# A two-layer block with routed experts on one core: the five hand-written step orders replaced, TensorE's fillers dropped

## The chip, the core and the metric

The kernel runs on one core of a Trainium2 chip. The metric is the device time of one execution in microseconds. The engines are TensorE (PE), VectorE (DVE), ScalarE (ACT), GpSimd (POOL) and SyncE (SP), which here only starts DMAs; each works through its own instructions in program order and meets the others at semaphores.

## What is computed

The input is 32 x 256 tokens of width 128 (8192 rows, float32). Six residual layers follow each other, each on the layer-normed sum so far:

```
x = x + 0.5 * ffn0(layernorm(x))     # 8 experts, top 2 of a softmax gate, plus a shared expert
x = x + attn0(layernorm(x))          # linear attention, 32 heads of 4, group norm
x = x + 0.5 * ffn0(layernorm(x))     # the same weights again
x = x + 0.5 * ffn1(layernorm(x))     # 8 experts, top 1
x = x + attn1(layernorm(x))          # gated recurrence over 256 tokens, 8 heads, rope
x = x + 0.5 * ffn1(layernorm(x))
```

The expert of ffn0 is `a = swiglu((x w1 + b1) * (x w3 + b3))`, `y = a w2 + b2`, and each token adds the y of its two experts, weighted by the gate.

## The kernel before

**Tiling.** x stays in the core's memory. It is cut into 16 chunks of 512 tokens (4 tiles of 128), and the chunks into three groups of 4, 6 and 6 for ffn0. A group's tokens are sorted by expert: POOL writes every token's row twice to a DRAM table (`scatter`, L1593, two indirect transfers a tile), at the places that the routing has counted. The table is then read in units of 512 sorted rows, four blocks of 128 that each have one expert: 10 units in group 0, 14 in groups 1 and 2. SP loads a unit by four transposing DMAs (`load_rows`, L1660) into one of five buffers `u_xp`; PE, ACT and DVE compute the unit; ACT copies its result and SP stores it to DRAM (L1677); POOL fetches two results for each token by indirect transfers (`fetches`, L1610, eight a chunk), into one of two buffers, and DVE adds them to x (`weighed`, L963).

**Steps.** The work is cut into steps, and each step has an index k that says which part of it an engine does. In this text: h l.c.k is step k of `head` for layer l (0 the first ffn0, 1 the attention and the second ffn0) and chunk c: in layer 1, k = 0 adds the fetched results and takes the statistics, 1 and 2 take the attention's mean and normalise by `rstd`, 3 to 10 are the attention, 11 on the second ffn0 (11 statistics, 12 normalise, 13 rows, 14 logits and half of the shared expert). In the layer's steps before ffn0 DVE's L920 and L924 make mean and variance, POOL's L1562 and L1564 make `rstd`, DVE's L931 normalises with it. r l.b.k is the routing of a pair of chunks (b), U l.g.u.k is unit u of group g: k = 1 and 2 are PE's products (L652, L659), which ACT widens and DVE multiplies (L1208, L1193, L1197), k = 3 is DVE's last product (L1201), k = 4 is PE's product with w2 (L670, L673), ACT's copy and SP's store. S l.g.t is a scatter, F l.c.n a fetch. The later layers are steps m and l (ffn1 before and after the second attention) and f and b (that attention, front and back).

**What sets the order.** Nothing in the loops does. The dictionary `turns` (L380) has a string for each of the five engines, a letter for each step; `order` (L513 on) takes for each letter the next step of its kind, and the engine's program does its part of that step, or nothing. Even units are u, odd ones w; heads a, b, c by chunk modulo 3. So an engine that meets a step whose input isn't there stands still, with all that its string has behind it. The letter z, on PE alone, is a filler: `warm` (L894) multiplies the identity by itself, 256 columns, into a place that nobody reads. The string before has 462 of them.

**SP's own steps.** At the start of a group (`experts`, k = 0 of unit 0) SP clears the ends of the experts' regions by eight small DMAs (L1645) and loads units 0, 1 and 2 in one step; k = 1 of unit u loads unit u + 3; k = 4 stores unit u. Before the load of unit 0 it waits for all scatters of the group (`scattered`) and for the cleared ends. `Waiting.wait_ge` remembers the highest value waited for on each semaphore and emits a wait only for a higher one.

Of the kernel before, what the change touches and what calls it, by code (L numbers as in the profile page):

```python
# [24 lines left out]
E = 8  # L25
# [110 lines left out]
def build(nc, dram, packed, x_in, out):  # L136
# [14 lines left out]
    with ExitStack() as ctx:  # L151
# [225 lines left out]
        for i, which in enumerate("abc"):  # L377
# [4 lines left out]
                "aazzzzzzzzzzzzzzzzzzzzzzzzzzzzzzzzzzzzzzzzzzzzzzzzzzzzzzzzzzzabbzzzzzzzzbcczzcaabbcaaarrrrbbbcbbbccc"  # L382
                "aaabbabbbaccczccaaarrrrrbbbcccbrrrbaaazzzzzzzzzzzzzzzzarrrrrbbbcccaccaaazzzzzzzzzzzzzzzzzzzuwrrrrrzz"
                "zzzzzuubbbwcccwuuzzzzzzzuzuwwaaazzwucccwwbbuuuwwuzwuwcuuwbbbuczauwwaucccwwzwuurrrrraazzzauubbbuwzzwa"
                "aarrrbzzzzzwzaabrrrrruuwbbbcccaaawcurrrrrcwwuuwwzzwcccaaauuawwawuurrrrrwuzwaaauuuuurrrwwwaaaawauuuaw"
                "bbbbauzzzzzzzzzzzzzzzzzzabaccccwwbubcazabuucwbucuuaaabbacazcwaazzawuubbbbbwwccuaaaabbbwarrrrrzzzwawc"
                "ccaucwwazzzcawuwcczcaauuzuwwwuaaauzaauuwaaawwrrrrrrrrzzzzzzzzzzzzzzzzzzzzzzuwwzzzuwuuuwuwzzuwwuwwuuw"
                "uwwwuuzzzwuuwbbbbubzzuwzzwzuwbbwbuuubccccaaaawbbcuwwucbbbcbwbcacuuwwbbbuwwccauuwawwacccuuucabbbzzbcu"
                "wwucccaawrrrrrbbaaauuwbawbccccabcwwaaazzubbcwuuwcwcuuubbbbbcwwuaaaaccubbbrrrrraawacccuuuwcwaabbbbzzc"
                "baaubcccbwwuaaawuzzzzzzubaabwwccccbbaaaucrrrrrwwczzzzzzzuuwbbbcwcbuurrzzzzzzzzrcbwbbzbaaaazauccawwuw"  # L390
# [11 lines left out]
            "vector": (
                "acbabacbcaabarabbrrbacarcbbabcbcacbrcbabcbrbbacbracarccbcrraarrcrbabcracrbabrcabrrrabcacrrbacrbarcuu"
                "uuccacwwwawcuuuuwwwwubwbbuuuubuccwwwbwcawracruuubuaurcbawwwwrarabrwauuuaucrrbuarcbrararcbrbrabwwwrra"
                "acwcwcarcruuuawwwuucwwaraarruuurrrwwwauuaaawwuuuarurbubaawwwbaccawacwuuubbaabubuaccbcabcabauuuubabca"
                "cauababaawwwcwbrawbrbbrcbcaacarcwwwwrwauuucacccauauawwwacwwaauuuuauaraarrrrwwwarrwwuuuuuwwwwwuuuuuww"
                "wrbwwuuucbuucbwwwwwabbuuuaubcbuabbwwwbwbbccwbbuuucbucubcbaacbwwwcwwbbccbuuuaucacwwwuawbcrwacrcacruuu"
                "caaruauabbcbrcwwwacbabwbwaabccaababcuuuuubcwwwbcawbrbwcrcbbrcuuucubaarcaucbrbwwwcaacbawabbcacabuuuwc"
                "acauubcbaacrbabrawwwrwbawbccrrbcbuuurucabcuabwwwrcbbrabcbwaawcccbauuucuabcurwwwcaccararcwaarbbwabacb"
                "rcabuuuabacbauwwwubabaccbwbcwacuuuuabbcrcubrcaabrbwwwccrawcwcruuuamcaucuaccwwwwamcuuuwaauaunnawwwwuu"  # L410
                "uuaurwaarararruuurrurwwwuwwmwwwuuuwwummunwwwmmmnnwmtmwmtmttttnnnmmuuunttnuwwwuwtttntwnttvtvuuuvvvvmm"
                "mluuttmwwwmttwwnnlmvtmtllttuuutuvunnnttvvvvonllltlowwwmmwwnuuuuuoovvnwwwtwuuunooovvvvulwtuoltttlltnn"
                "ttwwwtwwvlllvuuuluvvvvmmmoumotmwwwmwoowtmoootttuuuotuunnnttmmnwwwnwntwntvtmmmttvtmtmmvvvvttnnlttlmtl"
                "lttttnnnmmnvttvnnllltvvvvtonlovnnvttootttvvvvmmmllmttooonnnlltmtmvonnlllmvntltntmmvvvvtotmmmnnttottm"
                "tmtmootttvooomnnnottvttvvvvlvltnntmmttvtllnttvvvvnotlllommmnntlmmtmootmtttooonnnttvonnvnntvvvvltvltm"
                "mtnntttllnnnttnlllvttvvvvoltotmmmtmttvoottvttooovvvvtltlotvttllttvttlllvvvvototltvttoovtttooovvvvvvl"
                "lovvvvollooolllooolouw"
# [1203 lines left out]
        def sync_program(sp):  # L1621
            on = Waiting(sp)
# [373 lines left out]
```

## Time and profile before

| | |
|---|---|
| runs | 1545.92 us median of 3 (1544.52, 1545.92, 4823.48) |
| the profiled execution | 1546.17 us |
| its span, first to last instruction | 1544.2 us |
| mean granted TensorE clock | 0.922 of full |
| busy: PE, DVE, ACT, POOL | 84%, 75%, 48%, 43% |

The span is what the views below are made of; 1.97 us of the profiled execution lie around it. PE's records are matmuls whose ends are modelled, so a busy PE is not PE at its peak. Engines work in order: the number in square brackets behind a row is the time that the engine stood idle before it, and what it was released by. In a view by windows, each engine has its busy microseconds and its instructions in the stretch, then the granted clock, the DMA share and the GB/s.

### The profile page before, as it was taken

Reading aid. Unit: us, or ns where it says so; the run is one execution under the profiler, and the core shown is the slowest. Engines: PE = TensorE matmul, PEld = TensorE weight load, DVE = VectorE, ACT = ScalarE, POOL = GpSimd, SP = SyncE. Lnnn points to the kernel's source line nnn. Section 1 sums busy time; section 2 is a strip of 40 time slices with the busy share of each in tenths; the row PEclk is TensorE's granted clock in tenths of the full one; section 3 lists DMA queues with packets and bytes.
Section 4 is the critical chain, followed back from the end, with each engine's and each line's share of the span. In section 5 each row is a group of like instructions: output and inputs, shape, how many; then the busy total and the mean of one; then the engine's idle time right before and its main releaser. Section 6 shows DMA issues by size and latency. Waiting matters only on the chain.

```text
span 1544.2 us, 40929 instructions
## 1 busy us (share of the span) xinstructions
PE 1297.2 (84%) x15013; PEld 993.3 (64%) x15013; DVE 1153.2 (75%) x3632; ACT 737.0 (48%) x1226; POOL 671.2 (43%) x727
## 2 busy tenths in 40 slices
PE   1567987598876986888898899999998999999998
PEld 0434765476655765566676777777776776767776
DVE  5888698679746785788998675866678678787775
ACT  0344454235422443442554345565577547456572
POOL 0056646774457354766677514211235234130100
PEclk9987998799987988898999997999999989999999
DMA  8002423331133213321333321111111001000000
GB/s 279 0 30 68 111 60 93 101 92 52 62 93 104 71 48 82 82 65 51 95 92 100 80 72 53 38 43 49 36 39 31 21 22 32 16 20 9 9 16 22
DMA packets 171811, 94.21 MB, mean 61 GB/s; under 512 B 98411, under 2 KB 163078, under 8 KB 171366
## 3 DMA queue, kind: packets, MB, share of 16 engines
q1 hardware_dynamic: 151814, 54.19, 13.4%
q0 software_dynamic: 16384, 33.59, 7.4%
q10 hardware_dynamic: 3424, 3.81, 0.8%
q8 instruction: 130, 2.13, 0.6%
q14 instruction: 59, 0.48, 0.1%
HBM read 25.98 MB, written 45.61 MB: 46 GB/s over the span
## 4 chain that ended last, share of the span: by engine, by line
PE 44%; DVE 25%; issue 9%; POOL 7%; SPq 6%; ACT 5%; DMA 2%; POOLq 0%; DVEq 0%
PE bank L659 5%; SPq L1660 5%; PE bank L716 4%; POOL y_in L1610 3%; POOL rows L1593 3%; PE bank L693 2%; PE bank L743 2%; PE bank L673 2%; PE bank L530 2%; PE bank L873 2%; PE sums L890 2%; DVE heads_store L931 2%; PE bank L652 2%; DVE heads_store L1011 2%; DVE x L963 1%
## 5 line engine op out<-in xcount | busy, mean ns | idle before, releaser
L1610 POOL DMA_INDIRECT y_in<-ys,r_result x256 | 274.3, 1071 | 156.1 <-issue 69.5
L1593 POOL DMA_INDIRECT rows<-store,r_slot x256 | 262.7, 1026 | 106.4 <-issue 75.6
L659 PE MATMUL bank<-u_xp,w_hi 128*128 128x128 f16 x2432 | 252.6, 224 | 2.2 <-DMA u_xp<-rows 2.0
L659 PE MATMUL bank<-u_xp,w_lo 128*128 128x128 f16 x1216 | 232.0, 223 | 0.0
L659 PEld LDWEIGHTS bank<-u_xp,w_hi 128*128 x2432 | 198.7, 100 | 48.8 <-issue 9.0
L652 PE MATMUL bank<-r_member,by_expert 128*128 128x512 bf16 x304 | 120.0, 395 | 12.1 <-DVE u_linear_odd L1208 9.2
L659 PEld LDWEIGHTS bank<-u_xp,w_lo 128*128 x1216 | 121.4, 100 | 0.7
L963 DVE SCALAR_TENSOR_TENSOR x<-y_in,r_weight,x 128x128 f32<-128x128 f32 x256 | 72.6, 345 | 21.6 <-DMA y_in<-ys,r_result 20.5
L1407 ACT ACTIVATE heads_store<-bank,b3s,sc 128x512 f32<-128x512 f32 x64 | 49.4, 776 | 77.5 <-PE bank L530 77.0
L530 PE MATMUL bank<-heads_store,w_hi 128*128 128x512 f16 x256 | 82.8, 408 | 3.5 <-ACT u_linear_odd L1459 1.4
L716 PE MATMUL bank<-w_packed,heads_store 128*128 128x128 f32 x512 | 80.7, 303 | 0.9 <-DVE heads_store L1239 0.9
L1562 POOL TENSOR_SCALAR ve_last<-mv_last 128x4 f32<-128x4 f32 x16 | 3.8, 236 | 173.2 <-DVE mv_last L924 173.2
L716 PEld LDWEIGHTS bank<-w_packed,heads_store 128*128 128x128 f32 x512 | 74.0, 207 | 6.2 <-issue 1.8
L1562 POOL TENSOR_SCALAR ve_head<-mv_head 128x4 f32<-128x4 f32 x48 | 10.2, 212 | 143.2 <-DVE mv_head L924 141.5
L904 PE MATMUL sums<-w_ident_b 128*128 128x256 bf16 x362 | 57.4, 301 | 17.2 <-DVE own_region L1871 17.2
L931 DVE TENSOR_SCALAR heads_store<-x,mv_head,rstd_head 128x128 f32<-128x128 f32 x192 | 54.9, 359 | 22.3 <-POOL rstd_head L1564 22.3
L1379 ACT COPY heads_store<-bank 128x512 f32<-128x512 f32 x64 | 37.6, 587 | 69.1 <-PE bank L481 58.7
L693 PE MATMUL bank<-heads_store,f_w1s 128*128 128x512 f32 x128 | 69.5, 668 | 0.7 <-DVE heads_store L1228 0.6
L670 PE MATMUL bank<-by_expert,r_member 128*128 128x128 bf16 x304 | 32.3, 234 | 41.8 <-DVE u_linear_odd L1201 24.8
L1562 POOL TENSOR_SCALAR ve_front<-mv_front 128x4 f32<-128x4 f32 x16 | 3.1, 192 | 137.2 <-DVE mv_front L924 136.7
L1354 DVE TENSOR_TENSOR store<-store,bank 128x512 f32<-128x512 f32 x64 | 40.9, 680 | 27.2 <-PE bank L873 17.8
L1011 DVE SCALAR_TENSOR_TENSOR heads_store<-bank,b1s,heads_store 128x512 f32<-128x512 f32 x64 | 47.6, 744 | 12.7 <-ACT heads_store L1407 10.5
(340 smaller groups left out, 3468.1 us busy)
## 6 DMA issues: line engine op xcount, KB each, us to landing
ys<-u_y_even SPq DMA_DIRECT2D x38, 256.0 KB
ys<-u_y_odd SPq DMA_DIRECT2D x38, 256.0 KB
u_xp<-rows SPq DMA_TRANSPOSE x304
x<-x_dram SPq DMA_DIRECT2D x16, 256.0 KB, 7.2
rows<-store,r_slot POOLq DMA_INDIRECT x256, 2.3
y_in<-ys,r_result POOLq DMA_INDIRECT x256
out_dram<-x SPq DMA_DIRECT2D x16, 256.0 KB
rows<-blank SPq DMA_DIRECT2D x48, 64.0 KB, 1.6
```

The lines of the kernel that those rows point to most:

```text
L530: ins = pe.matmul(B[:], wp[:, m, :], s.xp[:, xp, :], start=(n == 0), stop=(n == 2))
L652: pe.matmul(B[:], by_expert[:, 2 * part + which, :], members(use).unsqueeze(2).broadcast_to([P, PER_UNIT, BLOCK]), start=True, stop=False, ...
L659: ins = pe.matmul(B[:, of_block[j]], of_expert(wp, e, 2 * part + which), xp_rows[:, xp, of_block[j]], start=False, stop=(n == 2 and j == P ...
L693: s.by_tensor.mark(pe.matmul(B[:], f1_w1s[:, j * P:(j + 1) * P], s.xt, start=True, stop=True), "gelu", c, j)
L716: pe.matmul(Y[:, by_t[t]], s.gs[j][:, by_t[t]], const["f1_w2"][:, j, :], start=(t == 0 and j == 0), stop=False, skip_group_check=True)
L904: pe.matmul(into, ident_b[:], ident_b[:, 0:HALF].unsqueeze(1).broadcast_to([P, T, HALF]), start=True, stop=True, skip_group_check=True)
L931: ins = dve.tensor_scalar(out[:, t, :], xc(c)[:, t, :], s.mv[:, t, 0:1], s.rstd[:, t:t + 1], ALU.subtract, ALU.mult)
L963: ins = dve.scalar_tensor_tensor(xt, y[:, t, i, :], w[:, i, t0 + t:t0 + t + 1], xt, ALU.mult, ALU.add)
L1011: s.by_vector.mark(dve.scalar_tensor_tensor(h, ring[s.name, "h", l, c, part, 1][:], b1s[:, part:part + 1], h, ALU.add, ALU.mult), "h", l, ...
L1593: pool.indirect_dma_start(row_dram[g], bass.IndirectOffsetOnAxis(route.slot[g][:, i, t:t + 1].bitcast(U32), 0), rows[:, groups[g].first * ...
L1610: pool.indirect_dma_start(fetch.y[i][:, t, k, :], None, y_dram[g], bass.IndirectOffsetOnAxis(route.result[g][:, k, t0 + t:t0 + t + 1].bitc ...
L1660: sp.dma_start_transpose(unit_xp[i % XP_BUFFERS][:, :, of_block[j]], block_rows(row_dram[g], firsts[j])).then_inc(rows_in[i % XP_BUFFERS], 16)
```

## The change

All five strings are replaced. A program that reads the letters as `order` does finds the same steps on each engine, each once, in another order: of the steps that have work on the engine, 654 of 890 stand at another place on PE (by 1.7 places in the mean), 883 of 1094 on DVE, 572 of 816 on ACT, 436 of 496 on POOL and 94 of 156 on SP. PE's string has 2 letters z where it had 462. And `load_rows` has its two waits at every unit:

```diff
-                if u == 0:
-                    on.wait_ge(scattered[g], 16 * 2 * groups[g].tiles * (l + 1))
-                    on.wait_ge(cleared[g], 16 * (1 + E * (l + 1)))
+                on.wait_ge(scattered[g], 16 * 2 * groups[g].tiles * (l + 1))
+                on.wait_ge(cleared[g], 16 * (1 + E * (l + 1)))
```

The strings, cut to the first lines of two of them:

```diff
             "tensor": (
-                "aazzzzzzzzzzzzzzzzzzzzzzzzzzzzzzzzzzzzzzzzzzzzzzzzzzzzzzzzzzzabbzzzzzzzzbcczzcaabbcaaarrrrbbbcbbbccc"
-                "aaabbabbbaccczccaaarrrrrbbbcccbrrrbaaazzzzzzzzzzzzzzzzarrrrrbbbcccaccaaazzzzzzzzzzzzzzzzzzzuwrrrrrzz"
+                "acaacburbbcaabaabccrbarbcbbbcarcrbaabcrcbaarbrabbraracbcrwbcabrrcrcbarcrbabcacaabrcbbrcrcuabuawruawc"
+                "urcauucwwwucbruwbubuwucrwbuwwubrcbcawwauawucuwaurarwrucbwrrwuawbuuacrubwcrcbaurrruacarwwawbbaraucrrw"
...
             "sync": (
-                "uuwwuuuuuwwwwwuuuwwwuuwwuuuuuwwwuuuwwwwwuuuuuuuwwwwwwwuuuuuwwwwwuuuuuwwwwwuuuuuwwwwwuuuuuuuuuuwwwwww"
+                "uuuwwwwuwuwuwuuuuwuwwuwuwwwuuuuuwwwuwuuowuwwuwwuwuwwuwwuwuouwuuuwwuuwuuuuuwwwuuwwuwwwuwowuwwwwwuuuu"
```

Read as steps with work, the places that the prediction speaks of (- before, + after; "load 0-2" is the step that clears and loads three units; "load 3" is U k = 1 of unit 0, and so on):

```
SP, start of group 1, layer 0   - load 0-2, load 3, store U0.0.9, load 4
                                + load 0-2, store U0.0.9, load 3, load 4
SP, start of group 2, layer 0   - load 0-2, load 3, store U0.1.13, load 4
                                + load 0-2, store U0.1.13, load 3, load 4
SP, start of group 0, layer 1   - load 0-2, load 3, store U0.2.13, load 4
                                + load 0-2, store U0.2.13, load 3, store U1.0.0
SP, start of group 1, layer 1   - load 0-2, store U1.0.9, load 3, load 4
                                + load 0-2, load 3, store U1.0.9, store U1.1.0
SP, start of group 2, layer 1   the same: load 0-2, load 3, store U1.1.13

POOL, F0.0.0 to F0.0.7          - 5 scatters of group 2 in between;  + 2
POOL, F0.7.0 to F0.9.7          - 8 steps of h, no scatter in between;  + 9 steps of h, 11 scatters
POOL, around F0.10.0            - S1.1.6 S1.1.7 h1.9.1 F0.10.0 h1.7.11 F0.10.1
                                + F0.9.7 S1.1.4 S1.1.5 h1.7.11 F0.10.0 ... F0.10.5 h1.9.1

DVE, end of group 1, layer 0    - U0.1.12.3 h1.3.15 r1.1.0 h1.3.16 h1.3.17 r1.1.1 r1.1.2 r1.1.3 r1.1.4
                                  U0.1.13.1 h1.3.18 r1.1.5 r1.1.6 U0.1.13.2 U0.1.13.3 U0.2.0.1
                                + U0.1.12.3 r1.0.4 h1.3.11 h1.2.17 h1.3.12 U0.1.13.1 h1.3.13 U0.1.13.2
                                  U0.1.13.3 h1.3.14 r1.1.0 h1.3.15 r1.1.1 h1.3.16 r1.1.2 U0.2.0.1
PE, the same place              - U0.1.13.2 r1.1.3 r1.1.6 22 fillers U0.1.13.4 3 fillers U0.2.0.1
                                + U0.1.13.2 h1.3.13 h1.3.14 U0.1.13.4 h1.3.15 h1.2.18 U0.2.0.1
DVE, first fetches of group 1   - U0.2.3.1 r1.1.7 h1.4.0 U0.2.3.2 U0.2.3.3 U0.2.4.1 h1.5.0 h1.4.1 U0.2.4.2
                                + U0.2.3.1 h1.4.0 h1.4.1 U0.2.3.2 U0.2.3.3 h1.4.2 U0.2.4.1 U0.2.4.2
                                  U0.2.4.3 U0.2.5.1 h1.4.4 r1.1.6 h1.5.0
DVE, first fetches of group 0   - U0.1.2.3 h0.15.7 h1.0.0 h1.0.1 U0.1.3.2 U0.1.3.3
                                + U0.1.2.3 h0.15.7 h1.0.0 r0.7.4 U0.1.3.1 U0.1.3.2 h1.0.1 U0.1.3.3
```

## Rows read from the trace of the kernel before

**Rows 1.** The page: busy time of PE, and POOL's group of scatters.

```profile
PE 1297.2 (84%) x15013; PEld 993.3 (64%) x15013; DVE 1153.2 (75%) x3632; ACT 737.0 (48%) x1226; POOL 671.2 (43%) x727
...
L1593 POOL DMA_INDIRECT rows<-store,r_slot x256 | 262.7, 1026 | 106.4 <-issue 75.6
```

**Rows 2.** Busy time of each engine in two stretches: experts' part, later layers.

```profile
60.00:900.00 840.00, 673.46 (x6352) 515.51 (x6351) 643.34 (x2095) 359.82 (x540) 504.38 (x526) 0.90 0.28 76
900.00:1544.00 644.00, 611.31 (x8583) 468.77 (x8580) 470.53 (x1428) 374.78 (x683) 162.65 (x188) 0.94 0.11 30
```

**Rows 3.** The same columns for three stretches of 40 us.

```profile
280.00:320.00 40.00, 26.04 (x232) 21.18 (x231) 25.81 (x85) 8.41 (x14) 31.37 (x33) 0.77 0.36 96
440.00:480.00 40.00, 25.84 (x285) 22.49 (x286) 15.13 (x33) 9.74 (x16) 21.52 (x21) 0.79 0.44 111
600.00:640.00 40.00, 24.87 (x203) 18.24 (x200) 22.23 (x74) 14.46 (x22) 19.98 (x21) 0.74 0.33 78
```

**Rows 4.** PE's timeline: start, us, instruction; in brackets the idle time before.

```profile
302.30 0.61 PE L652 MATMUL bank<-r_member,by_expert 128*128 128x512 bf16 x1 [9.24 <-DVE u_linear_odd L1208]
...
427.63 0.28 PE L608 MATMUL bank<-r_inside,r_own 8*1 8x40 f32 x2 [6.22 <-DVE r_inside L1156]
427.85 4.38 PE L904 MATMUL sums<-w_ident_b 128*128 128x256 bf16 x22
...
470.92 0.61 PE L670 MATMUL bank<-by_expert,r_member 128*128 128x128 bf16 x4 [12.25 <-DVE u_linear_odd L1201]
485.48 0.59 PE L670 MATMUL bank<-by_expert,r_member 128*128 128x128 bf16 x4 [5.17 <-DVE u_linear_even L1201]
...
616.40 0.59 PE L572 MATMUL bank<-gmv_head,w_packed 128*128 128x2 f32 x2 [12.94 <-DVE gmv_head L1043]
```

**Rows 5.** SP's timeline around three starts of a group.

```profile
427.64 22.69 SPq L1660 DMA_TRANSPOSE u_xp<-rows  x16
450.37 0.58 SPq L1677 DMA_DIRECT2D ys<-u_y_odd  x1
...
586.19 22.21 SPq L1660 DMA_TRANSPOSE u_xp<-rows  x16
608.45 0.58 SPq L1677 DMA_DIRECT2D ys<-u_y_odd  x1
...
246.64 22.65 SPq L1660 DMA_TRANSPOSE u_xp<-rows  x16
```

**Rows 6.** POOL's timeline: two fetches that waited, and the step behind one.

```profile
453.67 1.11 POOL L1610 DMA_INDIRECT y_in<-ys,r_result  x1 [12.57 <-DMA ys<-u_y_odd]
...
611.75 1.12 POOL L1610 DMA_INDIRECT y_in<-ys,r_result  x1 [13.51 <-DMA ys<-u_y_odd]
...
613.22 1.03 POOL L1564 TENSOR_TENSOR rstd_head<-ve_head,half_neg 128x4 f32<-128x4 f32 x1
```

**Rows 7.** DVE's timeline: the first fetched results of group 1, the step at 614.

```profile
466.76 2.31 DVE L963 SCALAR_TENSOR_TENSOR x<-y_in,r_weight,x 128x128 f32<-128x128 f32 x8 [8.69 <-DMA y_in<-ys,r_result]
...
614.28 1.36 DVE L931 TENSOR_SCALAR heads_store<-x,mv_head,rstd_head 128x128 f32<-128x128 f32 x4 [13.13 <-POOL rstd_head L1564]
```

**Rows 8.** The fillers alone (PE, PEld): by stretch, and the longest run late.

```profile
60.00:900.00 840.00, 39.93 (x244) 24.77 (x242) 0.90 0.28 76
900.00:1544.00 644.00, 28.01 (x164) 16.21 (x164) 0.94 0.11 30
...
878.49 3.11 PE L904 MATMUL sums<-w_ident_b 128*128 128x256 bf16 x27
```

**Rows 9.** The chain that ended last: twelve matmuls at either clock.

```profile
63.23 2.61 PE bank L530 x12
...
621.68 4.87 PE bank L530 x12
```

**Rows 10.** The tile u_xp: the transposing loads, and PE's waits for them.

```profile
L1660 SPq DMA_TRANSPOSE u_xp<-rows x304: 1167/1170/2272, 139.2 to 1083.0; - x152
...
  DMA u_xp<-rows: 2.0, 2
```

More of the change, by code:

```diff
@@ L386, in build @@
[L386 to L390, printed above, removed]
@@ new lines, in build @@
+                "uuccbcwaaacurbabwrabcbwauuacwrbawbcawuuawccuabbwccrwbwbcurcabarbrbbcaawacbuwubuarwrcmcuaucaccbrwbccb"
+                "ucrrbwwabacabuuwaabawwbrcaabbucwuuucaubacubwcbcuwcarawacrrbuwwracuucuarcwwmbrbcuaucwawwcuuauawawcwau"
+                "wwrcuuaurauuwuawuaarwurwuwauwuwwnruruwwmnmmwuwmwmwunmmnwntnutmtwummntwtmuutwttttwutvmwtvtwwvmtuvutom"
+                "unvtmnttnwvuwutnvlwwontlntunuvumvuttmlnvvmtwlutmwtntvummntwwlnuuonlwvuvwoovwowuwuvlvoumulvutowlwnttu"
+                "ltluonwwtlwtttvvvvumlovwumvnuwwlwtouummomoonwwltomooututtnwmtwnwnunntutttmvmwwttmvmtvttvntmvnvtntmnt"
@@ L414, in build @@
[L414 to L417, printed above, removed]
+                "abcabacbcaabarabbwracbarubbrccbcbaaccbrbcabrabrbraabrcbararcbcarcrbrcbaccbracrcabrrabacrccrbcuuwuuaw"
@@ new lines, in build @@
+                "wwwbrcubuaucburwuuabbcwwwcawbruubcbcwuwabrwawurarwucuurrabuurwwwcuwuawraraubuarccrrbucraarrawwcarbcc"
+                "awuawrwuuuabracwurarcbuarwawrawuwcruuauarwuwawuawruaubwruabwaubwaccubbawcbuwaacuwbucbababcurauacbbcu"
+                "wbaaacuawcababaurwcarabwbwcawcabwcarbwuucccawawuuuawwwuruawuuracawwawwuaraurarucwuwruwwwrauurwawuuuw"
+                "ububwwbubwwuuwubrcwurbwcbwuubbucubuwawwbbacwubcbcaucwcbbubcbcwwawucwbucwabbcuawucwuwubucacwracwarbar"
+                "uacawuuracbcacbwwbwawucaubcababcraabbuwbwcubacwcbwrbcbubruawcubrubuwccaawabucracbwcuracawacbwbauauca"
@@ new lines, in build @@
+                "uacbcbcuarbawbcwaburacwawbubacbucabwwucrcwacrucabrwbrbccbacarwcurawbbuabauubucrwwarcrbucawacbwcbarbu"
+                "wabccwburuacacbuawabwbwacubauabcuabrucuwacbwcbrucruawccbwrcawcuruuabucumcwamcwawwauwuauuwawcwaauwwcu"
+                "uawruauurrrawuuunawunawrwurwrwwumnumnwwmmwumwmwwunmtmtwnmuntnmtmwtuttnmtwuwutttwtwnvmwnttvntvummvvnt"
+                "uuutmttwwuvlwlwlmvnwttluututnvlmnumvtutmtnwvvrnwtuvutlomwlouuwolnvwvumnowwnuvwwuoovouuvuvtltlwontwtu"
+                "tllnttwlmwtvulwnvwwmuluvvummvvotonlowwowmtwuuwoomottuotuttmnumwntwtmmntwnvttnmtvntmvtmvtvtvnlttltmnt"
@@ new lines, in build @@
+                "bucuuwwubwbcaubabrwwurcauwcwubcawruwbwarrabrucbuuuwwarwrurawcruacauurwubwruarruabawwrurrarcwccaacbcw"
+                "babaurwuwurcbawcruaurabrawwacruuwuwuawauawuwbuaabuwwawacauwawarbubrcaubuwucccbaacuabbbwruuccbaaburrw"
+                "accawuaabcaaabcruwbarwbwcaawbbuwacacwuraccwwuacuwwaarwcuarruuuuwuwcwwcawaauraabuwbawuuwuwawbwuuwwuba"
+                "uuarwwuuwbcuucwwbwuwaububbuwwbubuwwucwrccbububruwwbcrrbabcbnbwcwrcwcbaacuwbuwucuuwwcwaracccrabucaubl"
+                "uawubwuaubawaccwwrcbbbarwcuabcabcbwucrwarubwbuwcbabbbbcrrwawbuuuaacucacacbwbbuaacwuwcuracbccaaabauua"
@@ new lines, in build @@
+                "ltlnotmmnlnnnffotnfflnnlfmottfotltttollfoltmotltttfttotttfmtltmtfnnnffmtmftmmtflmnlmltnffftltntmmlno"
+                "lfnftnmftffftfnnfootlfoffmtfntaonolonnlfnntttotmlftftlfoftmlmmtfnfltfalfffattolnmnmfotmtnnmtobfotntf"
+                "afmmfmafofnfffmtmtntnlttmomntttffcoftmomontltfoflffoltbmonlttnffftlmtfoontnmtncmomttoomntfffmfltltft"
+                "mttnffntntfnflttaffttnollltmtttlmtmnoltntoltmnttltlotbltttottotalolcocbtlntttonotottttllolltmolltmom"
+                "oltlctltllotollnooonobtlotoooool"
@@ L458, in build @@
+                "uwwuwuwuuwwwuuouuwwwowuwuwwwwuwwwuuuwwouwluuwuwlullluuwuwulwwuwuwlulwowwuuuwlooooluwuoowwululouulwuo"
+                "uwwolwwolllwouwlowlowouullolllollolllllolllloolllooollololllooolollllooooolloolollooooooolollooooloo"
+                "oooolllo"
             ),
```

89 lines of the change are left out of this document (33 added, 56 removed).

## The prediction

> **What bounds the kernel now.** I read the page first: PE is busy for 84% of the span, DVE for 75%, both with idle time in them [rows 1]. A table by windows shows that this is a mean over two different kernels. From 900 us on PE is busy for 611.3 of 644 us: the later layers are bound by PE [rows 2]. From 60 to 900 us it is busy for 673.5 of 840 us and DVE for 643.3: nobody is full, and engines wait for one another [rows 2]. There PE stands idle for 840 - 673.5 = 166.5 us, and 39.9 us of what counts as busy are fillers [rows 8]. So the order of the steps can win time before 900 us, and leaving fillers out can win it behind.
>
> Then I looked for where PE's idle time lies. Three stretches of 40 us have PE at 25 to 26 us, and the granted clock there is 0.74 to 0.79 [rows 3]. PE's timeline names the waits in and near them: 9.24, 12.25, 5.17 and 12.94 us, and a fourth place with 6.22 us and a run of 22 fillers of 4.38 us behind it [rows 4]. Each comes after the last unit of one group while the next group's first units are loaded, and each names a DVE instruction, so I asked what DVE waited for. At 466.76 it had stood 8.69 us for fetched results, with the unit's products behind it in its string; at 614.28 it had stood 13.13 us for POOL's rstd [rows 7]. POOL in turn had waited 12.57 and 13.51 us for the store of the group's last unit, and the rstd at 613.22 stood right behind that waiting fetch [rows 6]. SP had that store behind 16 transposing loads, 22.69 and 22.21 us long [rows 5]. So the chain at a group's start is: SP's sixteen loads, the store, POOL's fetches, DVE's sum, the heads of the next layer. The loads as such don't hold PE up: in the whole span it waits 2.0 us for them [rows 10].
>
> **SP's waits at every load cost nothing.** In the new order too the step that loads unit 0 comes before every other load of its group, it has waited for the same two values, and the helper emits no wait that is covered. The hunk adds no instruction. If one came, SP would pass it at once, since the semaphores are full.
>
> **Stores ahead of load 3: 5.4 us at three places.** In three of five starts the last unit's store moves ahead of load 3. A load is four transposes, and sixteen take 22.69 us, so four take 22.69 x 4/16 = 5.67 us; the loads 5.2 to 5.7 us; I take 5.4 [rows 5, 10]. POOL has been idle since 453.67 - 12.57 = 441.1 us for the second of them, so its fetch starts 5.4 us earlier [rows 6]. At the fourth start (750 us) it is the other way round, the store 5.4 us later; no wait in the rows hangs on it, and I price it at 0, at most 5.4. The fifth is unchanged. At the first start (246.64) the store frees the fetches of chunk 0, and POOL has two scatter steps between these eight fetches instead of five: three fewer, two transfers each, at (262.7 + 75.6)/256 = 1.32 us, so 7.9 us [rows 1]. The wait of 9.24 us at 302.30 lies behind them [rows 4]. From below a gain here is 0 (another chain takes over at once), from above the whole 9.24; I take 6.
>
> **The root ahead of the waiting fetch: 13 us.** At 611.75 POOL's string has h1.7.11 behind F0.10.0, which waits for the store. Its input is DVE's mean and variance of chunk 7, which DVE had ended before 614.28 - 13.13 = 601; DVE and then PE stand for 13.13 and 12.94 us [rows 6, 7, 4]. In the new order h1.7.11 comes before F0.10.0, so the wait is gone from its path. What is late next is the second ffn0 of chunk 7, whose rows PE can transpose at once, and units 0 and 1 of the new group, both loaded. Bounds 5.4 (only the store's share) and 12.94; I take 11.
>
> **DVE's units ahead of the second fetch: 5.17 us, and the earlier start.** At 485.48 PE waits for U0.2.4.3, which DVE has behind h1.5.0, the sum of a chunk that isn't fetched yet. The new order has all of U0.2.4 before h1.5.0, and h1.4.1 and h1.4.2 right behind h1.4.0, so chunk 4's norm no longer waits for chunk 5's fetches. The wait of 12.25 us before stays in kind (U0.2.3.2 is still behind h1.4.0) but shrinks by the store's 5.4. Together 5.4 + 5.2 = 10.6; bounds 0 and 17.4 [rows 4]; I take 9, since chunk 4's work now meets the units in a shorter time.
>
> **Routing behind the last unit: 6 of 10.6 us.** At 421 to 432 DVE has eleven steps of routing and head between U0.1.12.3 and its last part of the unit; PE idles 6.22 us and spins 4.38 us [rows 4]. The new order puts them behind. The next group's loads can't come earlier by this, as SP starts them behind another store; but head work that lay before the gap is now done in it. Bounds 0 and 10.6; I take 5.
>
> **The fillers left out.** A run of 27 takes 3.11 us at full clock, 0.11 each behind the first [rows 8]. Behind 900 us, where PE is the bound, 164 of them hold it for 164 x 0.11 = 18 us; before 900 they stand in time that is idle anyhow. Where a filler run ends just as the next input comes it costs nothing, so bounds 0 and 18; I take 9. What the fillers give is a high clock. The rows have its price: the same twelve matmuls took 2.61 us at 63.23 us, at the full level of 2.4 GHz, and 4.87 us at 621.68 us, at 1.2 GHz, shortly behind the idle wait of 12.94 us [rows 9, 4]. Without fillers some runs more will start low; with the long waits shortened some fewer. I let these two cancel and keep the difference for a rival.
>
> The Trainium skill speaks against this edit: "TensorE: Matmul & The Clock Gate", section "HAM oscillation — how this bites in real kernels", says in my words that waits between bursts of matmuls let the gate throttle again, so that every burst starts cold, and advises to keep PE going through them. The trace agrees as far as that pair of durations and the 0.74 to 0.79 of the three stretches go [rows 9, 3]; that these fell although the string has 462 fillers says that the fillers don't stand where PE really waits.
>
> **The sum.** 6 + 11 + 9 + 5 + 9 = 40 us, plus 4 for the matmuls that run at the high level once the waits are shorter (of the stretches' 56 us at the low level, found as 2 x (1 - clock) x 40, perhaps a seventh, half of it won [rows 3]). The profiled execution took 1546.17 us (span 1544.2, 1.97 around it), 0.25 above the median of the runs, so I take 1546: 1546 - 44 = **1502 us**. What a measurement of this kernel can tell from no change is about 2%, 31 us; faster by more is 1515 and less.
>
> **Rivals.**
> A. *The gain is caught at once by the next chain.* For it: DVE is at 77% before 900 us and PE at 80%, every engine in order, and 883 of DVE's 1094 steps have moved; in the new order POOL has 11 scatters, 22 transfers of 1.32 us = 29 us, between the fetches of chunks 7 to 9, where it had none, and POOL's idle time there may not hold them [rows 1]. Against: POOL is busy 504 of 840 us [rows 2]. Then only the 13 us wait goes: 1546 - 13 = 1533 us.
> B. *All of it comes.* The four waits whole, 9.24 + 12.25 + 5.17 + 12.94 + 10.6 = 50 us, the fillers' 18, and the low clock of the three stretches gone: 56 us at half rate, with PE busy 64% of it, cost 56 x 0.64/2 = 18. 1546 - 86 = 1460 us. Against: a fetch still needs its store, so part of each wait must stay.
> C. *The clock falls without fillers.* The mean granted clock is 0.922. Each 0.01 less is 2 x 0.01 x 1544 = 31 us more at the low level, and as PE is busy 84% of them, 13 us of PE's work; behind 900 us all of it, before it perhaps none, so half: 6.5 us. The gain of 44 us is eaten at a mean of 0.922 - 0.068 = 0.854; at 0.82 the time is 1546 - 44 + 66 = 1568 us. Slower than before begins below 0.854. For it: the rows on the clock; against: only 164 of the fillers lie where PE is the bound, and there the clock is 0.94 with PE hardly idle.
> D. *The change does nothing at the starts*, because a store isn't ready when its new place comes. The store of U0.1.13 waits for PE's product at 432 [rows 4], before the loads end, so this holds for none of the three; no chance of its own.
>
> **How the numbers follow.** My forecast 0.50 (own range 1486 to 1524), A 0.25, B 0.13, C 0.12. The range of 1458 to 1556 leaves out most of C and little else. Faster by over 2%: nearly all of B, five sixths of the forecast, a little of A: 0.58. Slower by over 2% (1577): the far end of C and of an order that fits the chip worse than the rows can show: 0.09. Within: 0.33.
>
> **What would show it.** In the changed profile: SP's store of the last unit behind twelve transposes, not sixteen, at three starts; POOL's waits for ys at 5 to 10 us where they were 12.6 and 13.5; no DVE wait for rstd over 5 us at the start of layer 1's units; PE busy over 30 of 40 us there; the later layers' stretch shorter by about 9 us with its clock at 0.92 or more. It is wrong if the clock's mean falls under 0.89, if the later layers take longer than 644 us, or if the part before them isn't at least 20 us shorter.

## The result, and the profile after

The changed kernel takes 1391.5 us (median of 4 runs, 1384.4 to 1393.4) against 1545.6 us: ratio 0.901 [0.897, 0.906], 154 us less. The prediction was 1502 us, range 1458 to 1556. It had the direction and missed the size by more than its whole gain. One execution of the kernel before took 4823 us and is left out of the ratio. The profiled execution took 1393.4 us, span 1391.5, mean granted clock 0.953 (0.922 before).

Line numbers of the kernel after are 4 or 5 lower than before (L1660 is L1655, L670 is L666). The page, for [rows 1]:

```profile
PE 1212.4 (87%) x14553; PEld 926.7 (67%) x14553; DVE 1152.7 (83%) x3632; ACT 726.0 (52%) x1220; POOL 685.5 (49%) x727
```

DVE does the same 1153 us of work in a span that is 153 us shorter. PE's busy time fell by 84.8 us. Fillers were 76.1 of these: 67.9 from 60 us on [rows 8], and 8.2 in the first 60 us, where PE has little else to do. The fillers alone there, before:

```profile
0.00:60.00 60.00, 8.17 (x56) 6.55 (x57) 1.00 0.58 180
```

The view by windows for [rows 2], columns as there. The border between the experts' part and the later layers now lies near 800 us; by PE's instructions the two halves hold the same work but for 21 matmuls, some 2 us, that now lie ahead of the border (8398 behind it; before 8583, of which 164 fillers):

```profile
60.00:800.00 740.00, 637.70 (x6129) 483.06 (x6126) 645.41 (x2111) 362.31 (x545) 512.28 (x523) 0.94 0.33 86
800.00:1391.00 591.00, 570.05 (x8398) 440.78 (x8396) 468.32 (x1415) 361.24 (x672) 169.09 (x192) 0.96 0.13 33
```

Read against [rows 2, 8], this says where the time went. PE's idle time is the window less busy; its own work is busy less fillers.

| us | experts' part, before and after | later layers, before and after |
|---|---|---|
| length | 840, 740 | 644, 591 |
| PE idle | 166.5, 102.3 | 32.7, 21.0 |
| fillers | 39.9, 0 | 28.0, 0 |
| PE's own work | 633.5, 637.7 | 583.3, 570.1 |

So of 153 us, 76 were idle time, 68 were fillers, and 9 a shorter time for PE's own work. The 9 come from the later layers alone, where the clock rose from 0.94 to 0.96; in the experts' part it rose from 0.90 to 0.94, and PE's own work didn't get shorter (637.7 us, some 2 of them from behind the border, against 633.5). The prediction looked at five long waits, 45.8 us in all [rows 4]. After, no wait of PE in this part is longer than 3.6 us. The waits in PE's view of the experts' part, most first (what is waited for: us in total, times, longest):

```profile
PE bank L514 <- DVE heads_store L993: 14.6, 10, 3.6
PE bank L485 <- DVE store L976: 14.1, 11, 3.1
PE bank L501 <- ACT heads_store L1378: 7.8, 9, 1.1
PE bank L666 <- DVE u_linear_odd L1197: 7.6, 4, 3.1
```

At the starts of groups, SP's timeline has what the prediction said, the store behind twelve transposes at three starts, for [rows 5]:

```profile
224.61 17.88 SPq L1655 DMA_TRANSPOSE u_xp<-rows  x12
242.54 0.58 SPq L1672 DMA_DIRECT2D ys<-u_y_odd  x1
...
380.81 16.80 SPq L1655 DMA_TRANSPOSE u_xp<-rows  x12
397.66 0.59 SPq L1672 DMA_DIRECT2D ys<-u_y_odd  x1
...
510.00 17.57 SPq L1655 DMA_TRANSPOSE u_xp<-rows  x12
527.62 0.58 SPq L1672 DMA_DIRECT2D ys<-u_y_odd  x1
...
656.41 23.38 SPq L1655 DMA_TRANSPOSE u_xp<-rows  x16
```

POOL's longest wait for a store is 5.8 us (12.6 and 13.5 before at the second and third start [rows 6], and 15.0 once behind 910 us), and DVE waits 2.2 us at most for POOL's rstd (13.1 before [rows 7]). From POOL's timeline:

```profile
532.57 1.13 POOL L1606 DMA_INDIRECT y_in<-ys,r_result  x1 [5.79 <-DMA ys<-u_y_odd]
```

and from DVE's waits:

```profile
DVE heads_store L927 <- POOL rstd_head L1560: 9.4, 10, 2.2
```

But the same transposes also show that the starts are not the main part. They began at 246.6, 427.6, 586.2 and 750.1 us before; the last of these rows, which [rows 5] doesn't have:

```profile
750.07 16.42 SPq L1660 DMA_TRANSPOSE u_xp<-rows  x12
```

At the first of them, ahead of every place that the prediction priced, the new order is 22.0 us early already; then 46.8, 76.2 and 93.7 us. The gain grows by 18 to 29 us a group. Equal windows around three starts, before:

```profile
246.00:310.00 64.00, 42.26 (x433) 32.99 (x431) 43.20 (x135) 21.95 (x34) 44.75 (x47) 0.83 0.36 98
427.00:490.00 63.00, 41.03 (x410) 34.42 (x411) 28.50 (x78) 13.27 (x22) 39.18 (x40) 0.77 0.38 98
586.00:640.00 54.00, 38.43 (x323) 28.98 (x321) 35.13 (x116) 19.79 (x30) 26.54 (x28) 0.81 0.31 75
```

and after:

```profile
224.00:288.00 64.00, 56.49 (x567) 42.52 (x566) 59.03 (x186) 29.62 (x45) 45.71 (x45) 0.95 0.35 93
380.00:443.00 63.00, 53.22 (x541) 42.49 (x540) 47.30 (x147) 24.17 (x39) 41.49 (x42) 0.93 0.48 108
510.00:564.00 54.00, 45.26 (x393) 35.08 (x392) 46.57 (x162) 23.30 (x37) 38.34 (x41) 0.94 0.30 76
```

DVE is busy for 153 of 181 us there, where it was for 107, and PE for 155 where it was for 122. Whether that is the starts' doing, or the order around them had put work ready for them, the profile can't say. The experiments are about this.

### The profile page after: what moved, and what is told of

Its sections match the earlier page's. It is cut to its first block, busy times and chain, and to the rows that moved or that the text cites. A ratio compares the mean times of both kernels' runs of the same rounds, so it can differ in the third digit from the quotient of the medians.

```text
span 1391.5 us, 40033 instructions
## 1 busy us (share of the span) xinstructions
PE 1212.4 (87%) x14553; PEld 926.7 (67%) x14553; DVE 1152.7 (83%) x3632; ACT 726.0 (52%) x1220; POOL 685.5 (49%) x727
## 4 chain that ended last, share of the span: by engine, by line
PE 46%; DVE 21%; issue 8%; POOL 8%; SPq 8%; ACT 5%; DMA 3%; POOLq 0%; DVEq 0%; ACTq 0%
PE bank L655 6%; SPq L1655 6%; POOL rows L1589 4%; PE bank L712 4%; PE bank L689 3%; PE bank L669 2%; POOL y_in L1606 2%; PE bank L869 2%; PE bank L648 2%; DVE heads_store L927 2%; PE sums L886 2%; PE bank L526 2%; PE bank L739 2%; PE bank L681 1%; PE bank L783 1%
## 5 line engine op out<-in xcount | busy, mean ns | idle before, releaser
L1606 POOL DMA_INDIRECT y_in<-ys,r_result x256 | 280.8, 1097 | 86.3 <-issue 70.8
L1589 POOL DMA_INDIRECT rows<-store,r_slot x256 | 266.5, 1041 | 93.6 <-issue 73.4
L655 PEld LDWEIGHTS bank<-u_xp,w_hi 128*128 x2432 | 190.5, 98 | 50.7 <-issue 8.3
L648 PE MATMUL bank<-r_member,by_expert 128*128 128x512 bf16 x304 | 116.8, 384 | 7.1 <-issue 1.6
L712 PE MATMUL bank<-w_packed,heads_store 128*128 128x128 f32 x512 | 80.9, 303 | 1.2 <-DVE heads_store L1235 1.1
L1558 POOL TENSOR_SCALAR ve_head<-mv_head 128x4 f32<-128x4 f32 x48 | 13.2, 274 | 105.2 <-DVE mv_head L920 103.0
L1350 DVE TENSOR_TENSOR store<-store,bank 128x512 f32<-128x512 f32 x64 | 40.9, 680 | 23.1 <-PE bank L869 12.3
L485 PE MATMUL bank<-ident_h,store 128*128 128x128 f16 x256 | 22.5, 241 | 40.0 <-DVE store L976 38.8
L514 PE MATMUL bank<-w_packed,heads_store 128*128 128x128 f32 x256 | 41.2, 309 | 14.6 <-DVE heads_store L993 14.6
L1560 POOL TENSOR_TENSOR rstd_head<-ve_head,half_neg 128x4 f32<-128x4 f32 x48 | 51.7, 1077 | 4.0
```

The lines of the kernel that those rows point to most:

```text
L648: pe.matmul(B[:], by_expert[:, 2 * part + which, :], members(use).unsqueeze(2).broadcast_to([P, PER_UNIT, BLOCK]), start=True, stop=False, ...
L655: ins = pe.matmul(B[:, of_block[j]], of_expert(wp, e, 2 * part + which), xp_rows[:, xp, of_block[j]], start=False, stop=(n == 2 and j == P ...
L712: pe.matmul(Y[:, by_t[t]], s.gs[j][:, by_t[t]], const["f1_w2"][:, j, :], start=(t == 0 and j == 0), stop=False, skip_group_check=True)
L1560: s.by_pool.mark(pool.tensor_tensor(s.rstd[:], s.ve[:], half_neg[:], ALU.pow), "rstd", which, c)
L1589: pool.indirect_dma_start(row_dram[g], bass.IndirectOffsetOnAxis(route.slot[g][:, i, t:t + 1].bitcast(U32), 0), rows[:, groups[g].first * ...
L1606: pool.indirect_dma_start(fetch.y[i][:, t, k, :], None, y_dram[g], bass.IndirectOffsetOnAxis(route.result[g][:, k, t0 + t:t0 + t + 1].bitc ...
```

## The experiments

"Old" and "new" are the orders before and after. In mixed kernels each step is in the old or the new order by the time at which it ran in the profile of before, on all five engines alike; nothing is added or left out but fillers. Ratios are to the kernel before on the same chip (1544.6 to 1547.5 us, the slow chip below apart).

**Fillers and halves.** The first question was whether gain came from order or fillers, and from which half.

```diff
old_nofill     PE's string of before
-462 letters z
new_fill       PE's string of after
+460 letters z, ahead of the same steps as before
new_then_old   all engines
-old order before 900 us
+new order before 900 us, no fillers there; behind it old order with 164 fillers
old_then_new   the other way round
```

> The orders of before with all 462 fillers taken out of TensorE's string, nothing else changed. Theory 'order' (the new orders themselves take the 154 us off, by less standing in line on every engine): the fillers stood mostly in idle time, so 1530 to 1548 us. Theory 'fillers' (they held TensorE up and a good part of the gain is theirs): 1490 us or less. Theory 'clock' (the fillers kept the clock up): slower than 1560 us with a mean granted clock of 0.88 or less.

> The new orders with 462 fillers put back, each run of them ahead of the same TensorE step that it stood ahead of before. Theory 'order': between 1392 and 1430 us, since TensorE has less idle time to hide them in; at 0.11 us each all of them are 51 us, those behind the experts' part 18 us. Theory 'fillers': 1450 us or more. If the clock gains by them, under 1392 us.

> All steps that had started before 900 us in the trace of before (the experts' part) in the new order without fillers; all later steps in the old order with their 164 fillers. The two profiles put about 100 of the 154 us into the first part. Theory 'each part by itself': 1440 to 1450 us. Theory 'the first part sets the second' (an earlier and better-filled start is what makes the later layers 50 us shorter): 1400 us or less.

> The reverse: the experts' part in the old order with its fillers, the later layers in the new order without. Theory 'each part by itself': 1546 - 50 = 1490 to 1500 us. Theory 'the first part sets the second': 1530 us or more. Of the 50 us, 18 would be the fillers of that part and the rest its order.

| kernel | median us | ratio [95%] | mean clock |
|---|---|---|---|
| old_nofill | 1561.6 | 1.010 [1.007, 1.014] | 0.900 |
| new_fill | 1406.4 | 0.911 [0.906, 0.917] | 0.961 |
| new_then_old | 1450.2 | 0.937 [0.933, 0.941] | 0.938 |
| old_then_new | 1499.2 | 0.969 [0.964, 0.974] | 0.929 |

The halves add up: 94 us for the experts' part and 45 us for the later layers, 140 of the 154, the rest within the intervals. The fillers have both signs. Leaving them out of the old order costs 17 us; putting them into the new order costs 15 (12 by the second measurement of the changed kernel, below). In the old order they stood in gaps and kept the clock up (0.922 to 0.900 without them; *old_nofill* so lies 14 us above the range of the theory 'order', with a higher clock than the theory 'clock' wanted). In the new order there are fewer gaps, and the clock is high without them (0.953 without, 0.961 with). *new_fill* by windows:

```profile
60.00:800.00 740.00, 654.87 (x6376) 499.06 (x6373) 644.25 (x2106) 362.31 (x545) 508.62 (x522) 0.95 0.33 86
800.00:1400.00 600.00, 582.94 (x8556) 454.68 (x8555) 469.33 (x1417) 360.45 (x672) 168.97 (x192) 0.97 0.13 33
```

PE is busy for 30 us more than in the changed kernel and idle for 21 less, so about a third of what the fillers take there isn't idle time. The Trainium skill ("TensorE: Matmul & The Clock Gate", section "HAM oscillation — how this bites in real kernels") says that waits between bursts of matmuls throttle the clock, and advises to rearrange the loop so that PE stays warm; it has no word on dummy matmuls. Both pairs agree as far as the clock goes: it fell by 0.022 without fillers in the order with the long waits, and the rearranged order has 0.953 without any. Where the waits are short already, the fillers' own time outweighs the 0.008 of clock that they add.

**Two chips with stalls of their own.** Four kernels met a chip on which the kernel before takes 1801 us (chip 7 in the record), and, measured again, another on which it takes 1797 us (chip 0). Each edit is shown where it is read, below.

> The kernel before with only the moves that the prediction named: SP's store of the last unit ahead of load 3 at three group starts, POOL's h1.7.11 ahead of F0.10.0, DVE's h1.4.1 ahead of U0.2.3.2 and U0.2.4.2 and 3 ahead of h1.5.0, and the routing r1.1.3 to 6 behind U0.1.13.3 (its two PE steps behind U0.1.13.4). All fillers stay. Named waits bound the time (the prediction's terms 6 + 11 + 9 + 5 = 31 us): 1508 to 1520. The next chain catches each gain, because DVE behind it is as late: 1535 to 1545, nothing that can be told from before. Half and half would be 1525 to 1533.

> The kernel before, with the new order of all five engines only for the steps that ran in three stretches around the group starts with the long waits (246 to 312, 420 to 492 and 580 to 642 us, 200 us together); the rest in the old order with its fillers. If the gain of the experts' part (94 us in the run with the new order before 900 us alone) comes from the waits at the starts: 1470 to 1495. If it is spread evenly over that part: 200/840 of 94 = 22 us, 1516 to 1528. If the starts profit only when the work around them is reordered too: 1535 or more.

> The other half: the new order of all five engines before 900 us except in those same three stretches, which stay in the old order with fillers; the later layers in the old order. To be held against the run with the new order in all of the experts' part (1450). Gain from the starts' waits: 1500 to 1520, most of the 94 us lost. Gain spread evenly: 94 x 640/840 = 72 us kept, 1468 to 1478. Starts and rest independent: what this one gains and what the other one gains add up to 94.

> The new order before 900 us, the later layers in the old order with their 164 fillers left out. Beside it stand 1450 us (the same with the fillers) and 1391 us (the later layers in the new order, without fillers). If the later layers gain because fillers held PE: 1425 to 1440. If they gain by the order alone and the fillers held the clock up for it: 1450 to 1470, with the clock of the stretch behind the experts' part lower than with them.

> The kernel of all_named again, on another chip if possible: where it ran, the kernel before itself took 1801 us, with stalls of up to 37 us on engines whose input was there, so a term of 31 us could not be read. On a chip where the kernel before takes 1545 us: named waits bound the time, 1508 to 1520; the next chain catches each gain, 1535 to 1545.

> The kernel of starts_new again, for the same reason. Gain of the experts' part from the waits at the starts: 1470 to 1495. Spread evenly: 1516 to 1528. Starts worth nothing unless the work around them is reordered too: 1535 or more. The first look (1797 against 1801 us, both disturbed) makes the last the likeliest.

> The kernel of starts_old again, for the same reason, beside 1450 us for the new order in all of the experts' part. Gain from the starts' waits: 1500 to 1520. Spread evenly: 1468 to 1478. If the starts are worth something only together with the work around them, this one keeps less than its share of the 94 us while starts_new_b gains little: 1480 to 1510 beside 1535 or more.

> The kernel of late_old_plain again, for the same reason. Fillers held PE in the later layers: 1425 to 1440. The order alone, with the fillers holding the clock up: 1450 to 1470.

| kernel | ratio on chip 7, on chip 0 | ratio on a chip with 1546 us |
|---|---|---|
| all_named | 1.001, 1.004 (±0.005) | 0.983 |
| starts_new | 1.000, 0.998 (±0.004) | 1.012 |
| starts_old | 0.985, 0.989 (±0.005) | 0.961 |
| late_old_plain | 0.970, 0.973 (±0.008) | 0.943 |

The last column is from runs told below. PE's timeline of all_named_b shows what was different: simple transposes of 0.27 us start at multiples of 0.71 us, and no other engine is named as the cause; DVE stood idle for 14.6 us meanwhile:

```profile
273.59 0.27 PE L488 MATMUL bank<-ident_h,store 128*128 128x128 f16 x1 [0.84 <-issue]
274.31 0.26 PE L488 MATMUL bank<-ident_h,store 128*128 128x128 f16 x1 [0.45 <-issue]
275.73 0.27 PE L488 MATMUL bank<-ident_h,store 128*128 128x128 f16 x1 [1.15 <-issue]
276.44 0.27 PE L488 MATMUL bank<-ident_h,store 128*128 128x128 f16 x1 [0.45 <-issue]
277.86 0.29 PE L488 MATMUL bank<-ident_h,store 128*128 128x128 f16 x1 [1.15 <-issue]
```

In the whole trace PE waits 74.7 us at the unit's matmuls with no releaser in the profile. On the chip of all_named_c that wait isn't in the list. From PE's waits:

```profile
PE bank L658 <- issue: 74.7, 90, 3.0
```

All four effects shrank, to half or to nothing. That such stalls cover part of the waits that an order could win back would explain it, but is not shown; nor is the late arrival of instructions that two expectations below speak of. A narrow interval there (all_named) would have been read as "the named moves give nothing", which is not so on another chip. These eight runs decide nothing further on.

**The starts of groups alone.** Three stretches of the old trace, 246 to 312, 420 to 492 and 580 to 642 us, hold the long waits.

```diff
starts_new     all engines
-old order in the three stretches
+new order in the three stretches
```

> The new order in the three stretches around the group starts alone. If the kernel before takes 1545 us on this chip: gain from the starts' waits, 1470 to 1495; spread evenly, 1516 to 1528; nothing without the work around them, 1535 or more. If it takes 1800 us, as where PE got its instructions one by one 0.7 us apart: a ratio of 0.97 or less for the first, 0.98 to 0.99 for the second, over 0.99 for the third, by the ratio that the whole change has there.

> The changed kernel as it is, as the measure for the run beside it. On a chip where the kernel before takes 1545 us: 1391, ratio 0.90. On one where it takes 1800 us: if the change's gain is waits for data between engines, and the instructions' late arrival adds to both kernels alike, the same 154 us, 1646 and ratio 0.915; if the late arrivals hide a part of the waits, less, ratio 0.93 to 0.96.

new_again took 1397.3 us, 0.903 [0.898, 0.908]: the whole change is the same here. starts_new_c took 1561.7 us, **1.012 [1.006, 1.018]**: the place of nearly all the priced terms, reordered alone, is slower. (35 of the 462 fillers are missing in the stretches; the mean clock of the profile is 0.923, as before.) It trades the named waits for others, from PE's timeline:

```profile
251.75 0.39 PE L657 MATMUL bank<-u_xp,w_hi 128*128 128x128 f16 x2 [5.14 <-DMA u_xp<-rows]
325.15 1.11 PE L479 MATMUL bank<-w_packed,heads_store 128*128 128x128 f32 x4 [12.21 <-DVE heads_store L929]
438.82 0.39 PE L657 MATMUL bank<-u_xp,w_hi 128*128 128x128 f16 x2 [6.05 <-DMA u_xp<-rows]
520.41 0.58 PE L576 MATMUL bank<-gn_vv_head,w_packed 128*128 128x2 f32 x2 [16.77 <-DVE gn_vv_head L1051]
```

and from DVE's:

```profile
518.34 1.35 DVE L929 TENSOR_SCALAR heads_store<-x,mv_head,rstd_head 128x128 f32<-128x128 f32 x4 [16.98 <-POOL rstd_head L1562]
```

At 251.75 and 438.82 PE reaches a group's first unit before its rows are loaded. The two longest waits, at 325.15 and 520.41, have another source: the cut itself. The new order does some scatters later than the old one, and where a stretch ends, those that it left over must all follow at once. So POOL has S0.2.9 to S0.2.14 in a row ahead of h1.1.1, and S1.0.10 to S1.0.15 ahead of h1.6.1, the rstd that DVE waits for. Neither the old nor the new order has six scatters in a row there. The second heap is twelve transfers, of which the first and the last, and the rstd behind them:

```profile
495.21 1.00 POOL L1591 DMA_INDIRECT rows<-store,r_slot  x1 [0.30 <-issue]
...
509.38 0.98 POOL L1591 DMA_INDIRECT rows<-store,r_slot  x1 [0.30 <-issue]
...
517.26 1.04 POOL L1562 TENSOR_TENSOR rstd_head<-ve_head,half_neg 128x4 f32<-128x4 f32 x1
```

The two waits are 29 us of PE's time, twice what the kernel lost. So this run doesn't show that the new order of the starts is worth nothing or less by itself.

**The named moves, the rest, the middle, the later layers.**

```diff
all_named      old order, with fillers
-SP: load 3, store U0.0.9 (the same for U0.1.13 and U0.2.13)
+SP: store U0.0.9, load 3 (the same for U0.1.13 and U0.2.13)
-POOL: F0.10.0 h1.7.11
+POOL: h1.7.11 F0.10.0
-DVE: h1.4.0 U0.2.3.2 U0.2.3.3 U0.2.4.1 h1.5.0 h1.4.1 U0.2.4.2 U0.2.4.3
+DVE: h1.4.0 h1.4.1 U0.2.3.2 U0.2.3.3 U0.2.4.1 U0.2.4.2 U0.2.4.3 h1.5.0
-DVE: r1.1.3 r1.1.4 U0.1.13.1 h1.3.18 r1.1.5 r1.1.6 U0.1.13.2 U0.1.13.3
+DVE: U0.1.13.1 h1.3.18 U0.1.13.2 U0.1.13.3 r1.1.3 r1.1.4 r1.1.5 r1.1.6
-PE: r1.1.3 r1.1.6 22 fillers U0.1.13.4 3 fillers U0.2.0.1
+PE: 22 fillers U0.1.13.4 3 fillers r1.1.3 r1.1.6 U0.2.0.1
starts_old     all engines, before 900 us
-old order
+new order, but old with fillers in the three stretches
late_old_plain as new_then_old
-164 fillers behind 900 us
mid_new        all engines
-old order from 246 to 900 us
+new order from 246 to 900 us
```

> The kernel of all_named on a chip where the kernel before takes 1547 us: all the moves that the prediction named, in the old order. Named waits bound the time: 1510 to 1522. The next chain catches each gain: 1540 to 1552. After starts_new_c (1562, slower than before by 1.2%) the second is the likelier.

> New order before 900 us except in the three stretches around the starts. The stretches alone cost 14 us (starts_new_c). If starts and rest are independent, this one gains 94 + 14 = 108 us: about 1437. If the new order of the rest makes the waits at the starts short by itself: 1440 to 1455, with the waits of 12 us there under 5 us. If the starts pay only together with the rest: 1475 to 1515, with waits of 9 to 13 us still there.

> New order before 900 us, later layers in the old order without fillers. Beside it: 1450 with the 164 fillers there, 1391 to 1397 with the new order. Fillers held PE: 1425 to 1441. The order alone, and the fillers held the clock up: 1450 to 1470. Neither: 1445 to 1455.

> The new order from 246 to 900 us only, the first 246 us and the later layers in the old order with fillers. The new order had group 0's last unit 18 us earlier than the old one. If every stretch gains by itself, this one keeps 94 - 18 = 76 us: 1466 to 1476. If the first stretch's gain was only lead that the next ones would have had anyway: 1450 to 1460. If the middle needs the first stretch's order (heads worked ahead): 1485 or more.

| kernel | median us | ratio [95%] |
|---|---|---|
| all_named_c | 1524.0 | 0.983 [0.975, 0.991] |
| starts_old_c | 1485.2 | 0.961 [0.954, 0.968] |
| late_old_plain_c | 1458.0 | 0.943 [0.935, 0.950] |
| mid_new | 1468.0 | 0.948 [0.941, 0.955] |

*all_named_c* gains 22 us (14 to 39 by its interval), where the prediction summed 31 for these terms. (The fewer scatters between the first fetches, a part of its first term, are not among the moves.) It lies 2 us above the range for named waits that bound the time; that I called the other one likelier after starts_new_c was wrong. The four rows of SP show where it comes in:

```profile
246.76 17.60 SPq L1659 DMA_TRANSPOSE u_xp<-rows  x12
...
422.20 16.11 SPq L1659 DMA_TRANSPOSE u_xp<-rows  x12
...
573.88 16.75 SPq L1659 DMA_TRANSPOSE u_xp<-rows  x12
...
729.50 16.85 SPq L1659 DMA_TRANSPOSE u_xp<-rows  x12
```

Against 246.6, 427.6, 586.2 and 750.1 us, it is 0, 5.4, 12.3 and 20.6 us early (the profiled execution, the longest of the four, ends 17 us early). So the first start gave 5.4 us (6 taken), the second with the units and the routing 6.9 (9 + 5 taken), the third with the root 8.3 (11 taken). What is left of the waits of [rows 4, 6], from PE's timeline:

```profile
459.83 0.61 PE L669 MATMUL bank<-by_expert,r_member 128*128 128x128 bf16 x4 [6.76 <-DVE u_linear_odd L1200]
608.12 0.60 PE L582 MATMUL bank<-row_bias,w_ones_b 3*128 3x512 bf16 x1 [5.70 <-DVE heads_store L1010]
```

and from POOL's:

```profile
593.97 1.15 POOL L1609 DMA_INDIRECT y_in<-ys,r_result  x1 [6.75 <-DMA ys<-u_y_odd]
```

The wait of 12.25 us became 6.76, its 5.4 for the store gone, as priced; the one of 12.94 went, and one of 5.70 for the attention of the same stretch came in its place.

*starts_old_c* gains 61 us, which is in the range of "only together with the rest", but the sign given for it, waits of 9 to 13 us still there, didn't come. Although SP still has the store behind sixteen transposes, POOL waits 2.7 us at most for it at these starts, and PE's longest wait from the first start to the fourth is this one:

```profile
446.11 0.61 PE L666 MATMUL bank<-by_expert,r_member 128*128 128x128 bf16 x4 [5.47 <-DVE u_linear_odd L1197]
```

So the long waits go when only the work around the starts is reordered, and 61 of the 94 us come with it. The other 33 are lost with the stretches in the old order (35 fillers among them), without a long wait.

With the 14 that starts_new_c lost, the two make 47, where the new order in the whole part gives 94. The sum falls short by 47 us, but that isn't a measure of how much the starts and the rest need each other: each kernel has cuts at 246, 312, 420, 492, 580 and 642 us, and the heaps of scatters behind two of them are 29 us of waits in starts_new_c. A kernel with these heaps spread out again was not tried.

*mid_new* gains 78 us of the 94, so the first 246 us carry the other 16. At that border the new order was 22.0 us early (its expectation took 18, from the last unit of group 0), so most of that lead was kept to the end.

*late_old_plain_c*: beside 1450 us with the 164 fillers, 1458 without; the intervals of the two ratios overlap. With the new order behind them the same steps end at 1391 to 1397 us. So in the later layers the order alone is worth 61 to 67 us when no fillers stand there, and their absence alone nothing. The late stretch of new_then_old, by windows:

```profile
800.00:1448.00 648.00, 613.03 (x8530) 470.41 (x8529) 464.03 (x1400) 370.25 (x677) 161.29 (x186) 0.92 0.11 30
```

of late_old_plain_c:

```profile
800.00:1457.00 657.00, 615.16 (x8390) 471.13 (x8389) 464.18 (x1398) 369.04 (x676) 159.04 (x185) 0.89 0.11 29
```

and of old_nofill, whose border is the old one:

```profile
900.00:1558.00 658.00, 617.13 (x8432) 469.58 (x8430) 473.17 (x1432) 375.12 (x684) 161.62 (x188) 0.91 0.11 29
```

Without fillers the old order's late stretch has PE busy for 615.2 us at clock 0.89; the new order does as many matmuls (8390 and 8398) in 570.1 us at 0.96. Of the 66 us between the two windows, 45 are the same matmuls taking less time, and 21 idle time. With its fillers (26.0 us in this window) the old order has the same busy time, 613.0 us, as the clock's 0.92 gives back what they take. That is why leaving them out alone shows nothing. In the new order it does show, but not in full: all of them back cost 12 to 15 us.

## Why the prediction was wrong

**SP's waits at every load: nothing. Right.** The kernel before with the hunk has the same instructions on every engine, SP's waits among them, as without it; so has the kernel after without the hunk.

**Stores, root, units, routing: 31 us taken, 22 measured.** The mechanism held, in each of three starts. The sizes were 5.4 us against 6, 6.9 against 14 (units and routing) and 8.3 against 11: the middle one was taken at twice its size. Rival A (only 13 us, caught by the next chain) is beaten by this run, if not by far. The signs named for it all came in the changed kernel: twelve transposes, POOL's waits at 5.8 us, no long wait for rstd, PE busy for over 30 of 40 us.

**"So the order of the steps can win time before 900 us, and leaving fillers out can win it behind."** This sentence, and the sum that followed from it, is the step that failed. Behind 900 us PE was taken as the bound because it was busy for 611 of 644 us, and only the fillers were priced, 9 us (bounds 0 and 18). That part gave 53. Before 900 the sum had 35 us, 31 of waits and 4 for the clock of three stretches, and 100 came. The later layers' fillers were 28.0 us in the very row that the step cites, not 18; the matmuls there ran at a clock of 0.94, where 13 us more lay; and there were 33 us of idle time, of which 12 went. The same part gained 45 us with its order new and the part before it old, and leaving out its fillers alone gained nothing. The 4 us for the clock before 900 show nowhere: PE's own work there did not get shorter.

**"Before 900 they stand in time that is idle anyhow."** True, and it should have been carried on: 39.9 us of PE's busy time in the experts' part was idle time by another name, so an order can win it. With the idle time of 166.5 us that made 206 us open to a new order. The sum looked for its gain in the 45.8 us of long waits, and so did rival B, which was meant as the upper end: 50 + 18 + 18. Of the 120.7 us of idle time outside these waits it had nothing, and of the fillers' 40 only the one run of 4.4. The upper end for an order that is new everywhere is what every gap would give: 166.5 + 32.7 + 67.9 = 267 us from [rows 2, 8]. 144 of them came, and 9 by the clock. The range should have reached far below 1458.

**The moves were priced one at a time, in an old order.** 654 of PE's 890 steps moved, and the sum took those at five places, 31 us of the 100. starts_old_c shows what it left out: with none of the moves at the starts the experts' part gains 61 us, and the long waits are gone with them. Whether the places can be priced apart is open. At 900 us the parts add up; around the starts they don't (-14 and +61 us, but 94 together), and there the cuts made orders of their own, with 29 us of waits.

**Fillers: 9 us, the clock cancels.** Alone the sign was the other one, 17 us slower. The clock did fall, by 0.022, which is 14 us by rival C's 6.5 us for each 0.01. Less the 9 us taken for the fillers' own time that makes 5 us, so either that price was too low or the 9 weren't there. As a forecast for the whole change C was wrong, for the clock rose to 0.953 with the fillers gone; much of the idle time that pulls it down had gone too.

What stays open: which of some hundred short waits each move removes, and by which rule the new order was found, so that a reader could have told from the strings that it fits the chip better. Whether a few fillers at chosen gaps of the new order would help was not tried; all of them back cost 12 to 15 us.

## What to carry to other kernels

When a whole schedule is replaced, price the open time, not the moves: idle time of the engine that is busiest, plus its fillers, plus the work that ran at the low clock, each by stage, is the upper end of the gain, and the long waits that can be named are its lower part (22 of 154 us here). Fillers are a placeholder for missing work: whether they help depends on the order they stand in, so measure them again after each reordering, in both directions. And when a schedule's parts are tested apart, look at the ends of each cut before reading the result: a cut makes an order that neither schedule has, and what it leaves over can cost more than the part is worth.

## What the runs showed of the chip

Chips 7 and 0 ran the kernel before in 1801 and 1797 us instead of 1546, at a granted clock of 0.87. The kernels profiled there have matmuls that in places start 0.71 us apart, and stalls that no other engine in the profile explains (up to 15 us on PE, up to 40 us on ACT and DVE). The record names a different chip each time, with three others (14, 3 and 8) near 1546 us, so it isn't the fault of one; the cause is open. An edit worth 1.7% on chip 8 showed as 0 ± 0.5% on each of these two. I had not expected an effect of this size to vanish within so narrow an interval; the kernel before's own time, in the same table, is what gives this away.
